# Two attention layers around a mixture of experts: the scatters of the first layer issued in a row behind the two roots, one batch earlier, and the store of zeros issued behind the spreading of keys

## What is computed

```python
x = x + tanh(g_xattn[0]) * xattn0(layernorm(x), ctx, mask0)
x = x + tanh(g_ffn[0])   * moe(layernorm(x))        # top 2 of 8 experts, F = 1024
x = x + tanh(g_xattn[1]) * xattn1(layernorm(x), ctx, mask1)
x = x + tanh(g_ffn[1])   * fourier(layernorm(x))
```

## Time and profile before

| what | us |
|---|---|
| median of 3 runs | 1325.3 (1319.2 to 1327.23) |
| the profiled execution | 1330.37 |
| its span, first to last instruction | 1328.8 |
| PE (TensorE) busy | 1194.3 |
| DVE (VectorE) busy | 889.6 |
| ACT (ScalarE) busy | 570.9 |
| POOL (GpSimd) busy | 268.1 |

### The profile page before, as it was taken

How to read it: one execution, slowest core, us unless ns; L and a number is a source line. 1 busy time by engine, 2 the same in 40 slices (tenths; PEclk the granted TensorE clock), 3 DMA queues, 4 the chain that set the end, 5 groups by cost and what they waited for, 6 DMA issues and landing times.

```text
span 1328.8 us, 35096 instructions
## 1 busy us (share of the span) xinstructions
PE 1194.3 (90%) x11815; PEld 995.8 (75%) x11816; DVE 889.6 (67%) x2697; ACT 570.9 (43%) x1187; POOL 268.1 (20%) x414
## 2 busy tenths in 40 slices
PE   4897989898767999989999899999998899999996
PEld 3686767777556888868888788888887577777884
DVE  4696666667644667566675767666565787787773
ACT  4474555455423233242422424242223566666653
POOL 5023333332341000000000000000003334444410
PEclk9998787888868999999999999999999899999998
DMA  9444242333444213012131222211012222222210
GB/s 294 171 129 131 81 135 88 128 106 100 146 155 151 92 37 124 33 62 92 32 122 37 85 66 68 88 33 37 26 53 73 60 82 86 84 87 84 82 38 25
DMA packets 82755, 119.67 MB, mean 90 GB/s; under 512 B 27325, under 2 KB 52557, under 8 KB 80588
## 3 DMA queue, kind: packets, MB, share of 16 engines
q1 hardware_dynamic: 64172, 60.32, 14.6%
q0 software_dynamic: 12848, 49.05, 11.0%
q10 hardware_dynamic: 5616, 8.78, 1.8%
HBM read 63.81 MB, written 47.58 MB: 84 GB/s over the span
## 4 chain that ended last, share of the span: by engine, by line
PE 72%; issue 8%; DVE 6%; DMA 5%; POOL 3%; ACT 3%; SPq 2%; ACTq 2%; DVEq 0%; another core or an unknown queue 0%; POOLq 0%
PE bank L1775 25%; PE bank L1788 13%; PE bank L1602 6%; PE bank L1536 5%; PE bank L1458 5%; DMA expert_in<-h,slot 4%; PE bank L1589 3%; PE bank L1478 3%; PE bank L1519 3%; PE bank L1521 2%; PE bank L1542 2%; PE bank L1613 2%; PE bank L1600 1%; POOL rstd L646 1%; DVE x L1121 1%
## 5 line engine op out<-in xcount | busy, mean ns | idle before, releaser
L1775 PE MATMUL bank<-tiles,we 128*128 128x256 f16 (+1 forms) x3744 | 394.9, 259 | 5.6 <-issue 4.7
L1775 PEld LDWEIGHTS bank<-tiles,we 128*128 128x128 f16 x3744 | 325.7, 98 | 47.0 <-issue 13.2
L950 ACT ACTIVATE tiles<-bank 128x256 f32<-128x256 f32 (+1 forms) x312 | 109.3, 353 | 336.4 <-PE bank L1775 301.7
L1788 PE MATMUL bank<-we,tiles 128*128 128x256 f16 x1608 | 225.5, 274 | 20.5 <-DVE tiles L1388 19.6
L1384 DVE SCALAR_TENSOR_TENSOR tiles<-bank,tiles 128x256 f32<-128x256 f32 (+1 forms) x312 | 120.0, 384 | 164.1 <-ACT tiles L950 160.6
L1788 PEld LDWEIGHTS bank<-we,tiles 128*128 128x128 f16 x1608 | 148.1, 98 | 59.1 <-DVE tiles L1388 33.6
L1096 DVE TENSOR_REDUCE bm<-bank 128x4 bf16<-128x308 f32 x256 | 118.2, 475 | 78.6 <-PE bank L1521 70.3
L1536 PE MATMUL bank<-qT,kbd 128*128 128x256 f16 x960 | 158.3, 284 | 2.4 <-issue 1.2
L471 DVE TENSOR_TENSOR pr<-pr 128x512 f16<-128x512 f32 x160 | 108.4, 682 | 34.2 <-ACT pr L812 30.8
L1390 DVE TENSOR_TENSOR tiles<-tiles 128x256 f16<-128x256 f32 (+1 forms) x312 | 121.1, 388 | 11.8 <-DVE tiles L1388 1.3
L1536 PEld LDWEIGHTS bank<-qT,kbd 128*128 128x128 f16 x960 | 95.5, 102 | 21.8 <-issue 3.1
(11 more groups left out here) (198 smaller groups left out, 1740.9 us busy)
## 6 DMA issues: line engine op xcount, KB each, us to landing
expert_out<-zeros SPq DMA_DIRECT2D x16, 896.0 KB
wes<-in_guT POOLq DMA_DIRECT2D x9, 1024.0 KB, 5.2
tiles<-expert_in SPq DMA_DIRECT2D x29, 256.0 KB, 2.6
pr<-in_guT POOLq DMA_DIRECT2D x7, 1024.0 KB
yg<-in_dnT POOLq DMA_DIRECT2D x7, 1024.0 KB
expert_out<-tiles ACTq DMA_DIRECT2D x28, 256.0 KB, 2.1
expert_in<-zeros POOLq DMA_DIRECT2D x8, 640.0 KB, 12.8
xin<-in_x SPq DMA_DIRECT2D x16, 256.0 KB
```

The lines of the kernel that those rows point to most:

```text
L950: act.activation(ge[:, fc % 2, 0:n * P], bank[1 + fc % 3][:, 0:n * P], ACT.Gelu, scale=INV).then_inc(s.gelu, 1)
L1775: last = pe.matmul(bank[1 + fc % 3][:, half * S:half * S + w * P], gate_up[:, par, c, i, col:col + P], xT[:, j, c, 0:w * P], start=n == 0, ...
L1788: last = pe.matmul(bank[4 + t][:, 0:D], act16[:, fc % 4, i, t * P:(t + 1) * P], we[:, par, 2, j, fc * D:(fc + 1) * D], start=fc == 0 and n ...
```

## The change

GpSimd no longer scatters batch b-3 in pieces between its other work. From step 2 on, step b scatters batch b-2, all four in a row, behind both roots. What step 15 did for batch 13 alone becomes the rule, and batches 14 and 15 follow behind the last root as before. The waits for the mask and for the attended rows fall away in layer 0. In layer 1 GpSimd's gathers keep their places. On SyncE `clear(b)` moves from the end of the step to right behind `spread(b+1)`.

```diff
@@ step0, SyncE
                 if front:
                     spread(b.after(1))
+                clear(b)
                 if tail:
                     keep(b.after(-1))
...
                     load(b.after(3))
-                clear(b)
@@ step, GpSimd
-                late = b.layer == 0 and not (isinstance(b.i, int) and b.i < 3)
+                late = b.layer == 0 and not (isinstance(b.i, int) and b.i < 2)
                 part = ld and b.layer == 1
-                one = (lambda n: gather(b.after(3), n)) if part else (lambda n: scatter(b.after(-3), n))
                 if part:
                     wait_apart(pool, s.places_recalled, b.i + 4)
-                if late:
-                    scatter_ready(b.after(-3))
-                if late or part:
+                if part:
                     wait_apart(pool, s.mask_ready, b.n + 1)
-                    one(0)
+                    gather(b.after(3), 0)
                     if tail:
                         wait_apart(pool, s.attended_high, pv.n + 1)
-                    one(1)
-                    one(2)
+                    gather(b.after(3), 1)
+                    gather(b.after(3), 2)
                 if tail:
                     ln_root(1, s.root_after, s.variance_after, pv)
-                if late or part:
-                    one(3)
+                if part:
+                    gather(b.after(3), 3)
                 if pre:
                     root(b.after(2))
-                if b.layer == 0 and isinstance(b.i, int) and b.i == 15:
+                if late:
                     scatter_ready(b.after(-2))
                     for n in range(2 * QT):
                         scatter(b.after(-2), n)
```

## The result

The changed kernel takes 1256.9 us in the median of 4 runs (1254.7 to 1259.2), the kernel before 1326.3 (1319.2 to 1327.8): a ratio of 0.949, 95% interval 0.945 to 0.953. I had said 1247 in a range of 1239 to 1271. The profiled execution took 1257.2 us with a span of 1255.6; before, 1330.4.

A forecast was written before the change was run, and what follows sets the result against it. Layer 0 was taken as bound by TensorE waiting for late scatters, then running at a lowered clock. 76.7 + 1.5 = 78.2 us off the profiled 1330.4 gives 1252.2, as a median 1247, range 1239 to 1271.

The forecast's parts named there:

- the sum: Whole kernel: 76.7 us from layer 0's 13 steps plus 1.5 at its end, 78.2 us saved.
- The split between them: 54.9 and 21.8: Layer 0's 13 steps: of 76.7 us saved, 54.9 are ScalarE's waits for scatters and 21.8 TensorE's lowered clock.
- The median: Whole kernel: the median of the runs lies 5.1 us under the profiled execution, taking 1252.2 to 1247.
- 13 x 15.85: Layer 0's 13 steps: each takes 15.85 us after the change, 206.05 in all, against 282.75 before.
- The end of layer 0: Last stretch of layer 0, 369.06 to 384.68: part runs at the high clock, saving 1.5 us, bounds 0 and 3.
- GpSimd at nothing, cover 5.7 us: GpSimd's moved scatters: cost nothing, the fourth landing 5.7 us before the next step's `h2_norm` needs it.
- `nr` would not be late next: Layer 0's `h2_norm`, notably steps 14 and 15: once scatters are no longer awaited, the shift `nr` isn't late either.
- SyncE at nothing: SyncE's moved store of zeros and the key loads: cost 0, even if the store takes 5 us longer.
- the 3.95 us of the chain: Layer 0, step around 212: time from the fourth scatter's issue to its landing, in a queue shared with the zeros.
- Rival B: Layer 0's steps: wait goes, clock stays low; only 54.9 us saved, 17.5 a step, about 1270; 0.18 with another rival.

The follow-up runs named there:

- e4: The kernel before with 24 unused filler matmuls of 200 columns ahead of the turn of h2, every wait kept: 1306.7 us, ratio 0.983.
- e2: The kernel before with only the store of zeros, `clear(b)`, moved behind `spread`: 1282.8 us, ratio 0.963.
- e7: The changed kernel with 32 one-element GpSimd operations ahead of the row of four scatters: 1256.0 us.
- e6: The changed kernel with the 16 stores of zeros taken out of layer 0's steps and issued behind its last step: 1287.1 us.
- e5: The kernel of e1 with 16 one-element GpSimd operations ahead of the row of scatters: 1255.1 us, ratio 0.947.
- e1: The kernel before with only the scatters moved as in the change, the store of zeros left at the step's end: 1313.2 us, ratio 0.987.
- e9: The kernel of e5 with 8 one-element GpSimd operations in place of 16: 1315.3 us.
- e12: The kernel of e8 with five kinds of step (unchanged, no zeros, delayed row, gaps between scatters, zeros at step's end): 1307.9 us, ratio 0.982.
- e8: The changed kernel with steps 3 to 12 of layer 0 written out instead of looped: 1247.6 us, ratio 0.941.
- e11: The changed kernel with steps 3 to 12 of both layers written out: 1311.5 us.
- e3: The kernel before with the fourth scatter issued right behind the third, ahead of `ln_root`: 1276.2 us, ratio 0.959.

## Why the prediction was right, and where not

**The total and its mechanism.** Both causes are borne out: the wait is gone, and the clock came back. The profiled executions differ by 73.2 us, where the sum was 78.2.

**The split between them: 54.9 and 21.8.** This was off, and the sum did not notice, since it came from the lengths of steps. In the traces the 13 steps take 282.75 us before, 256.2 in e4, where the waits stay and the clock is back, and 210.4 after the change. So the clock is worth about 26.6 us and the waits 45.8, not 54.9. (In e4 the clock still sinks in the last two steps, and the medians alone, 17 to 28 us, would not decide.) A wait of ScalarE is not all on the path: in the step of the earlier trace rows ScalarE stands for 3.55 us but TensorE only for 2.29, since it has work of its own for the first 1.3 us. That is also why e2 pays only 0.9 us a step for waits of 2.02: its steps take 17.1 us against 16.3.

**The median.** Half of the miss of 9.9 us has nothing to do with the steps. I took 5.1 us off for the distance from the profiled execution to the median; after the change it was 0.3.

**The mis-sized term: 13 x 15.85.** The step is 16.19 us, 4.4 us more in all. I took the length from a written-out step, and the ten in the loop cost 0.5 more each. With the loop written out the mean is 15.79, within 0.1 of the forecast. A step inside the loop stood in the trace of before as well, but with its waits and the low clock mixed in.

**The end of layer 0.** From the last `h2_norm` but one to the last it is 14.97 us against 15.62, 0.65 less where I took 1.5; the clock is 0.77, since `h2_norm` waits 7.31 us for `nr` there and layer 0's matmuls run out.

**GpSimd at nothing, cover 5.7 us.** Right, and tested: e7 issues the row 5.63 us later without loss. That `nr` would not be late next holds for the ordinary steps and step 14; in step 15 it is waited for, 0.61 us. The 7.31 us before the last `h2_norm` are not new, they were 6.91 in the kernel before.

**SyncE at nothing.** Right for the changed kernel: e6's steps without any zeros are of the same length. By itself the move takes 1.65 us off each wait, where the prediction had some 1.7 from the 3.95 us of the chain and the Trainium skill's 2.3 (DMA: Bandwidth & Descriptors, section Anatomy of one DMA). In e2's chain a scatter lands 2.46 to 2.48 us after its issue, close to that figure. What I left out is that a wait so shortened no longer brings the clock down: that made the part alone worth 46.6 us. The two parts overlap, and their gains don't add: e2 has 46.6 us with the zeros moved alone, and e5 has the whole gain with the zeros where they were. The scatters' move alone, without e5's delay, was measured only in e1, with the stall.

**What no step of it held.** A program with the row of scatters behind the roots may run with steps of 20.5 us instead of 16.2, without any wait for a scatter. Five of the ten kernels with that row do (e1, e9 to e12), and five don't (the changed kernel, e5 to e8). The changed kernel was measured without the stall, so its 0.949 is the better of two cases. e11, which has its order and should be faster, gains only 1.5% over the kernel before (ratio 0.986, 0.982 to 0.989). Rival B, waits gone and the clock still low, had 17.5 us a step; this is dearer, and I had no row that could show it: GpSimd's scatters stood in the same trace with all engines at work.

**What stays open.** What puts a program into this condition, and what delays TensorE's signals in it. Not the order of the instructions (e8 and e11), not the zeros (e12's steps without them), and not the chip by itself, if the same number stands for the same chip (e12 and e5 to e8). For a condition of the group speaks that all the kernels with this row in one group are alike, four and three of them, and, weakly, that the median of the kernel before is 1326 to 1328 us in the groups without the stall and 1329 to 1332 in the others; its single runs overlap. For a condition of the program, where it lies in memory for instance, speaks that e3's ordinary steps, with the last three scatters 1.3 to 1.7 us apart but ahead of the root, take 16.0 to 16.7 us. (Its steps 14 and 15 have rows of four as close as in e1: behind the first, at 283 us, come its four late signals, behind the later ones none.) A third possibility is the recording of the trace: the five that stall hold 12,419 to 13,287 records of signals, the five that don't 15,185 to 15,814. Whether fewer records are an effect of the stall or have to do with its cause isn't shown. None of the kernels with this row was run in two groups, which would tell the first two apart. It follows that e1 and e5 can't be compared with each other, nor e1 with the changed kernel: my first reading, 56 us for the place of the zeros, fell with that.

## What to carry to other kernels

A late transfer costs its wait, less what the bounding engine can still do meanwhile, and then the clock behind it: here ScalarE's 54.9 us of waits cost about 46 and the clock some 27 more, and cutting each wait from 3.7 to 2.0 us was enough to keep the clock. Take the length of a step from the form in which it will run, since a loop costs its own share; and if an edit that should be neutral moves the time by several per cent, measure a kernel a second time, at another time and on another chip, before a mechanism is built on it. A row of indirect DMAs issued by GpSimd beside full engines is a risk of its own; with gaps between them it cost less when it went badly (e12, 16.8 to 17.0 us a step against 19.4 and more). And when several engines stand still together, look at what each waits for before calling it one stop: here it was one engine's signals.

## What the runs showed that I had not expected

While the data of a GpSimd scatter moved, results of TensorE were made known 1.1 to 1.5 us late, so that VectorE, ScalarE and then TensorE stood still, at a granted clock of 1.00 and with 238 GB/s on the DMA engines, in a program whose twin showed nothing of the kind at 230 GB/s. With scatters 1.3 us apart the steps were 4 to 5 us longer, with 2.9 us from one to the next 1.0 to 1.2.

The prediction weighed a rule of the Trainium skill (GPSIMD Engine Reference, section Specifications) by which GpSimd and VectorE contend for SBUF. These traces neither bear it out nor refute it for the scatters: the second one takes 1.37 us in e8, beside VectorE's operation with two SBUF inputs (line 475, at 86.96), and 0.98 in e11, while VectorE stands still; but e11's third takes 0.96 beside the same operation, at 85.77. The stall itself the rule doesn't explain, since VectorE then waits for TensorE's signal and is not at work.

In layer 0 a loop of two steps costs 0.5 us a step more than the same steps written out (16.28 against 15.77), in layer 1 only 0.1 (17.38 against 17.28).
